# GpSimd computes the inverse square roots of the normalisations, in place of ScalarE's root and VectorE's reciprocal

## The reference

```
ln(x) = (x - mean) / sqrt(var + 1e-5)
x = x + tanh(g0) * cross_attention(ln(x), ctx)      # first attention, 16 heads
x = x + tanh(g1) * moe_64_experts(ln(x))            # top 8 of 64 experts, and a shared one
x = x + tanh(g2) * mlstm(ln(x), ctx)                # 16 heads; each head's output is normalised
                                                    #   h * rsqrt(var(h) + 1e-6) * scale
x = x + tanh(g3) * block(ln(x))                     # block: a = h + attention(ln(h)*w1+b1),
                                                    #   a + moe_4_experts(ln(a)*w2+b2)
```

## Time and profile before

| | |
|---|---|
| runs | 1759.97 us median of 3 |
| profiled execution, its own time | 1760.46 us |
| its span (first to last instruction) | 1759.2 us |
| TensorE busy | 1610.3 us, 92% |
| VectorE, ScalarE, GpSimd busy | 1101.2, 1007.2, 609.9 us |
| mean granted clock of TensorE | 0.946 of full |

### The profile page before, as it was taken

The page is one execution under the profiler, slowest core; times in us unless marked ns, Lnnn a source line. Parts: engine busy times, 40 slices in busy tenths (PEclk is TensorE's granted clock), DMA queues, the critical chain, the costliest instruction groups (busy, mean ns, idle before and its releaser), DMA issues.

```text
span 1759.2 us, 30253 instructions
## 1 busy us (share of the span) xinstructions
PE 1610.3 (92%) x10996; PEld 1269.9 (72%) x10996; DVE 1101.2 (63%) x2052; ACT 1007.2 (57%) x2050; POOL 609.9 (35%) x495
## 2 busy tenths in 40 slices
PE   4589999699999999999996984999999999999898
PEld 2245655388888888888872553788888888888687
DVE  6668886577544455444445566866876777666554
ACT  4368888444433344333335663877877876776543
POOL 5333333133435333333430002454454464443000
PEclk9589999899999999999995896999999999999899
DMA  5646665264433333334300003344344334332310
GB/s 157 194 143 200 205 203 161 88 148 111 108 105 105 107 113 107 105 105 115 112 9 8 4 2 128 104 149 162 114 139 122 123 121 134 121 115 67 72 49 25
DMA packets 111028, 196.16 MB, mean 112 GB/s; under 512 B 16712, under 2 KB 59532, under 8 KB 108064
## 3 DMA queue, kind: packets, MB, share of 16 engines
q1 hardware_dynamic: 110880, 194.21, 36.6%
HBM read 167.64 MB, written 25.73 MB: 110 GB/s over the span
## 4 chain that ended last, share of the span: by engine, by line
PE 78%; DVE 7%; ACT 5%; issue 4%; DMA 2%; POOL 2%; SPq 1%; ACTq 0%; POOLq 0%; DVEq 0%
PE bank L67 17%; PE bank L69 17%; PE bank L68 17%; PE bank L262 4%; PE bank L304 4%; PE bank L290 3%; PE bank L1790 3%; PE bank L1758 3%; PE bank L1780 1%; POOL e_hidden L1008 1%; PE bank L1290 1%; PE bank L1289 1%; PE bank L1300 1%; PE bank L1309 1%; PE bank L1754 1%
## 5 line engine op out<-in xcount | busy, mean ns | idle before, releaser
L1008 POOL TENSOR_TENSOR e_hidden<-e_gated,e_comb_wide 128x512 f32<-128x512 f32 x132 | 211.2, 1600 | 347.7 <-DVE e_gated L973 332.0
L848 ACT CAST e_hidden_hi<-e_hidden 128x512 fp32r<-128x512 f32 x132 | 82.0, 621 | 319.2 <-POOL e_hidden L1008 319.2
L966 DVE TENSOR_TENSOR e_hidden_lo<-e_hidden,e_hidden_hi 128x512 fp32r<-128x512 f32 x132 | 98.1, 743 | 212.1 <-ACT e_hidden_hi L848 212.1
L69 PE MATMUL bank<-e_x_hi,e_weights_lo 128*128 128x512 f32 (+1 forms) x528 | 209.8, 397 | 0.0
L67 PE MATMUL bank<-e_x_hi,e_weights_hi 128*128 128x512 f32 (+1 forms) x528 | 208.8, 395 | 0.7 <-ACT e_comb_rows L808 0.7
L68 PE MATMUL bank<-e_x_lo,e_weights_hi 128*128 128x512 f32 (+1 forms) x528 | 208.8, 395 | 0.0
L1869 ACT ACTIVATE b_turned<-bank,b_swap_bias 64x512 f32<-64x512 f32 x256 | 175.1, 684 | 44.0 <-PE bank L69 40.5
L481 DVE TENSOR_REDUCE a_negmax<-bank 128x2 f32<-128x512 f32 x256 | 164.5, 684 | 42.4 <-PE bank L262 41.2
L2018 POOL TENSOR_TENSOR b_turned<-b_turned,b_rope_q 128x512 f32<-128x512 f32 x64 | 82.7, 1292 | 255.8 <-ACT b_turned L1869 255.8
L398 ACT ACTIVATE a_exp<-bank 128x512 f32<-128x512 f32 x256 | 143.8, 596 | 30.1 <-PE bank L290 21.5
L69 PE MATMUL bank<-e_weights_hi,e_hidden_lo 128*128 128x256 f32 (+1 forms) x528 | 149.0, 282 | 0.0
(11 more groups left out here) (327 smaller groups left out, 4133.3 us busy)
## 6 DMA issues: line engine op xcount, KB each, us to landing
e_comb_wide<-e_combT SPq DMA_DIRECT2D x130, 256.0 KB, 4.0
e_raw<-in_e_weights SPq DMA_DIRECT2D x64, 384.0 KB, 4.5
b_qk_hi<-b_qk_parts SPq DMA_DIRECT2D x64, 256.0 KB, 2.7
b_qk_lo<-b_qk_parts SPq DMA_DIRECT2D x64, 256.0 KB, 3.0
a_qs<-a_q_parts SPq DMA_DIRECT2D x48, 192.0 KB
a_ks<-a_k_parts SPq DMA_DIRECT2D x48, 192.0 KB
b_qk_parts<-columns SPq DMA_DIRECT2D x32, 256.0 KB, 3.5
b_vw_hi<-b_v_parts SPq DMA_DIRECT2D x16, 512.0 KB, 4.1
```

Source lines behind the costliest of these rows:

```text
L69: return pe.matmul(out, w_lo, x_hi, start=False, stop=stop, skip_group_check=True)
L966: dve.tensor_tensor(lo[0:rows, :], m.hidden[at % 2][0:rows, :], hi[0:rows, :].bitcast(F32), ALU.subtract).then_inc(s.hidden_lo)
L1008: pool.tensor_tensor(m.hidden[i][0:rows, :], m.gated[i][0:rows, :], m.comb_wide[u % E_RING][0:rows, chunk * BANK:(chunk + 1) * BANK], ALU. ...
```

## The change

24 roots move: four of the router's norms, two column norms, two of the mLSTM's norms, four of the cells' factors (128x64), eight first and second norms of the block's attention and four of its gates. ScalarE's square root and VectorE's reciprocal go; GpSimd computes t to the power -0.5 in place, against a constant column of -0.5 that is spread over the free dimension. The semaphores keep their names: `root` now means that the inverse root is done, and is raised by GpSimd. The four norms ahead of the first attention stay as they are.

```
+def inverse_root(k, t):
+
+    return k.nc.gpsimd.tensor_tensor(t, t, k.minus_half[:, 0:1].to_broadcast([P, t.shape[1]]), ALU.pow)
 def layer0_pool(k, m, s, ring):
+    pool.memset(k.minus_half[:, :], -0.5).then_inc(own.tick())
 # experts_act, route and columns (the same in scan_act, cells_act, gate_act, attention_act)
-        if piece == 1:
-            act.wait_ge(s.var, chunk + 1)
-            act.activation(t.norm.rstd[:, :], t.norm.rstd[:, :], ACT.Sqrt).then_inc(s.root)
 # experts_dve, norm_end (the same in scan_dve, cells_dve, norm_end_dve)
-        dve.reciprocal(t.rstd[:, :], t.rstd[:, :]).then_inc(own.tick())
-        dve.wait_ge(own.sem, own.n)
 # experts_pool
+    def root(chunk):
+        pool.wait_ge(s.var, chunk + 1)
+        inverse_root(k, m.routers[chunk % HALF].norm.rstd[:, :]).then_inc(s.root)
     pool.wait_ge(before.added, NB)
+    for chunk in range(HALF):
+        root(chunk)
     for n in range(len(E_STEPS)):
         for chunk in range(HALF, NCHUNK):
+            if route_piece(chunk, n) == 1:
+                root(chunk)
+        for chunk in COLUMNS_AT:
+            if column_piece(chunk, n) == 1:
+                pool.wait_ge(s.column_var, chunk + 1)
+                inverse_root(k, m.columns_norm.rstd[:, :]).then_inc(s.column_root)
 # scan_pool
     pool.memset(first(w.drop), LOWEST).then_inc(s.resets)
+    for i, chunk in enumerate(LEFT):
+        pool.wait_ge(s.var, i + 1)
+        inverse_root(k, w.norms[chunk].rstd[:, :]).then_inc(s.root)
     pool.memset(m.log_gate[0:PARTS, :, :], 1.0).then_inc(s.log_ready)
 # cells_pool, for each group g, behind the weighing of its cells
+        pool.wait_ge(s.rooted, g + 1)
+        inverse_root(k, m.factor[g % 2][:, :, :].rearrange("p b h -> p (b h)")).then_inc(s.deviation)
 # gate_pool
+    if piece == 1:
+        pool.wait_ge(s.gate_var, chunk + 1)
+        inverse_root(k, m.norm.rstd[:, :]).then_inc(s.gate_root)
 # attention_pool
+        if piece in (1, 4):
+            pool.wait_ge(s.var, 2 * chunk + (piece == 4) + 1)
+            inverse_root(k, w.norm.rstd[:, :]).then_inc(s.root)
-    pool.wait_ge(s.small_in, 4 * DMA)
-    for piece in range(6, INPUT_PIECES):
+    for piece in range(INPUT_PIECES):
+        if piece == 9:
+            pool.wait_ge(s.small_in, 4 * DMA)
         input_chunk(0, piece)
```

More of the change, by code:

```diff
@@ L834, in experts_act @@
             piece = column_piece(chunk, n)
-            if piece == 1:
-                act.wait_ge(s.column_var, chunk + 1)
-                act.activation(m.columns_norm.rstd[:, :], m.columns_norm.rstd[:, :], ACT.Sqrt).then_inc(s.column_root)
             if piece in (3, 4):
@@ L1149, in scan_act @@
         keys_act(k, m, s, piece)
-    for i, chunk in enumerate(LEFT):
-        act.wait_ge(s.var, i + 1)
-        act.activation(w.norms[chunk].rstd[:, :], w.norms[chunk].rstd[:, :], ACT.Sqrt).then_inc(s.root)
     for half in range(2):
@@ L1351, in cells_act @@
         g, piece = divmod(n - M_LATER, CHUNK)
-        if g >= 0 and piece == 2:
-            act.wait_ge(s.rooted, g + 1)
-            act.activation(m.factor[g % 2][:, :, :], m.factor[g % 2][:, :, :], ACT.Sqrt).then_inc(s.deviation)
         if n < NB:
@@ L1420, in cells_dve @@
             dve.wait_ge(s.deviation, g + 1)
-            dve.reciprocal(factor[:, :, :], factor[:, :, :]).then_inc(own.tick())
-            dve.wait_ge(own.sem, own.n)
             dve.tensor_tensor(factor[:, :, :], factor[:, :, :], inv[:, :, :], ALU.mult).then_inc(own.tick())
@@ L1607, in gate_act @@
     act, cols = k.nc.scalar, slice(chunk * BANK, (chunk + 1) * BANK)
-    if piece == 1:
-        act.wait_ge(s.gate_var, chunk + 1)
-        act.activation(m.norm.rstd[:, :], m.norm.rstd[:, :], ACT.Sqrt).then_inc(s.gate_root)
     if piece in (3, 4):
@@ L1708, in norm_end_dve @@
 def norm_end_dve(k, t, src, dst):
-    dve, own = k.nc.vector, k.dve_steps
-    dve.reciprocal(t.rstd[:, :], t.rstd[:, :]).then_inc(own.tick())
-    dve.wait_ge(own.sem, own.n)
+    dve = k.nc.vector
     for b in range(CHUNK):
@@ L1833, in input_chunk @@
         cols = slice(chunk * BANK, (chunk + 1) * BANK)
-        if piece in (1, 4):
-            act.wait_ge(s.var, 2 * chunk + (piece == 4) + 1)
-            act.activation(w.norm.rstd[:, :], w.norm.rstd[:, :], ACT.Sqrt).then_inc(s.root)
         if piece in (6, 7):
@@ L2210, in program @@
         k.ident, k.gates = (stack.enter_context(nc.sbuf_tensor(n, s, F32)) for n, s in (("ident", [P, P]), ("gates", [P, 4])))
+        k.minus_half = stack.enter_context(nc.sbuf_tensor("minus_half", [P, 1], F32))
         k.columns_ready = [k.sem(f"columns_ready{chunk}") for chunk in range(NCHUNK)]
```

## The result

The changed kernel took 1776.49 us (median of 4 runs, 1768.84 to 1781.28) beside 1759.70 for the one before (4 runs, 1750.63 to 1762.73): ratio 1.0089, 95% interval 1.0052 to 1.0126. It is slower by 17 us. The forecast was 1734, and its range of 1726 to 1748 missed. The profiled execution took 1775.44 us for a span of 1774.1.

The account below looks back on a forecast made before the run. TensorE, busy 92% of the span, bounds the kernel; only its idle time or lowered clock counts. Terms -10.4, -12.5, +0.1, +0.2, -3.9, -0.7, +0.9 sum to -26.3 from 1760.5: forecast 1734 us, range 1726 to 1748.

Parts of the forecast that it names:

- its own price: Cost of a power on GpSimd, taken as ten multiplies per element: 1.5 us for 128x64, 0.5 for 128x4.
- slow rival: In the cells VectorE stands behind a slow 128x64 power; 1769 us at 10 us, decides from about 8 us; 7%.
- Inner groups: Cells: ScalarE goes straight to the exponentials, TensorE keeps 5.15 us steps and clock; -13.2, less 0.7 given back, -12.5 us.
- The lost clock: In the cells, with a 10 us power, each inner stall lowers the clock again, 2 us each.
- Last two groups: End of the cells, where nothing hides the power: +0.7 us each, less a load of 1.3 us; sum +0.1.
- First norms of the block: First two norms, TensorE idle: 0.5 us of power for a root and reciprocal of 0.2 each; +0.2 in all.
- Attention of the block: Roots and their table loads go, so TensorE's ten waits for the exponentials go; -10.4 us.
- what was to show it: Signs: 16 ScalarE loads, `b_probs` wait under 1 us, even cell steps at full clock, power near 1.5 us, others.
- The sign that was to warn: VectorE's L1423 waiting for GpSimd in the cells' inner groups would show the forecast wrong.
- Experts in the loop: Router norm's rows 1.5 us earlier: -2.2 us of TensorE waits, -1.7 of clock; sum -3.9.
- Ahead of the loop: First chunk's rows start earlier, without ScalarE in the chain, held by the first weights' split; -0.7 us.
- Start of the mLSTM: Powers push GpSimd's memset of `m_log_gate` among VectorE's rows, which end later; a loss of +0.9 us.

Follow-up runs that it names:

- experiments 2 and 4: 2: only the cells' four 128x64 powers, on the kernel before, 1791.84 us; 4: changed kernel plus spare operations ending GpSimd's stream, 1777.53 us in one run.
- experiment 1: Changed kernel with the cells' four 128x64 factors back on ScalarE's root and VectorE's reciprocal, the other 20 roots on GpSimd; 1742.84 us, ratio 0.989.
- experiment 3: Changed kernel with a GpSimd multiply in place of the cells' 128x64 power, leaving that root out; 1735.82 us, ratio 0.9857.
- experiment 6: Kernel before with only the roots of the block's attention and gates moved to GpSimd's power; 1749.86 us, ratio 0.9951.
- experiment 5: Changed kernel with the cells' power taken of half the tile, 128x32, leaving part of the root out; 1753.86 us, ratio 0.9965.

## Why the prediction was wrong

**The step that failed** is the first of "The change part by part", its own price: "I take ten multiplies per element, which is nearer the low rows: 1.5 us for 128x64". It is 96 multiplies and 10.52 us. No run shows how the power is computed inside. The range of the price did hold it (13 us for a hundred multiplies), and so did the slow rival, which puts its threshold at 8 us and got 7%. The estimate from the nearest rows was an estimate about another kind of operation: a multiply says nothing of what a power does per element, and "nearer the low rows" was no reason. With two bounds a factor of 40 apart and none of the middle shown, the case beyond 8 us deserved much more than 7%. That case was also said to want four times the multiplies taken; by its own figures, 60 against 10, it is six times.

The slow rival had the mechanism right: VectorE stands in order behind the power, most of it uncovered in the inner groups and all of it in the last. Its sum of 1769 us at 10 us becomes 1771 at 10.52 us; 1776.5 was measured.

The price goes into three terms. *Inner groups:* there are two of them and not the three of the prediction's heading (four in all, and the last two are counted apart); the sum went by the two long steps and isn't changed by it. The forecast hid 3.5 us of a power. Measured, 10.52 - 7.17 = 3.35, and with half the tile 5.41 - 2.06 = 3.35: that part was right. The lost clock, put at 2 us a stall, was 5.7 at the first and 1.6 at the second (13.89 us step, less 5.15 and 7.17), and 1.6 to 3.8 behind the same wait in experiments 2 and 4. The 13.2 us that were to be won here also came from one execution: its six steps took 44.1 us, those of experiment 1, with the same order, 40.7. *Last two groups:* 33.26 us against 12.78 with the multiply, a difference of 20.48, and 2 x (10.52 - 0.29) = 20.46 is the whole of it. *First norms of the block:* 1.01 us each in place of 0.5, so +1.2 and not +0.2.

**With the cells corrected the sum closes, in part by luck.** Cells and stretch behind them came to +27.9 for -12.4, 40.3 more; 1734.2 + 40.3 = 1774.5, and the profiled execution took 1775.4 (the median is 1776.5). But 4.4 us of the measured time are the first attention's, which the change doesn't touch, and they stand against the 3.3 us that the block's heads gave beyond their term. The better test is experiment 3: without the price it gives 1735.8, for a forecast of 1734.

**Attention of the block**, -10.4: right in the waits, and 0.9 to 3.3 too small in the whole, by busy time that goes with the waits (experiment 6). The measured waits were the better base: the estimate of some 20 us, from the drain that the Trainium skill (ScalarE: Activation LUTs, What ACT_TABLE_LOAD costs) adds to each load, doesn't agree with the 11.3 to 13.7 of the traces.

Of what was to show it, the 16 loads, the wait for `b_probs` (0.8 us in all) and the stretched rows came. The power near 1.5 us (10.52) and that of 128x4 near 0.5 (1.0 to 1.5), the even steps of the cells and the full clock there did not, nor did the wait of about 1 us for rows near 372, which went altogether. The sign that was to warn, VectorE's product behind the root (L1423, now L1426) waiting for GpSimd, came with 37.4 us in four waits, 16.1 of them in the inner groups.

**Experts in the loop**, -3.9: -3.9, but the tenth is luck. The waits for rows, 3.2 us, went altogether where 2.2 were booked, so 0.7 is left for the clock where 1.7 were booked. In experiment 6, with the experts' roots still on ScalarE, the first wait was 1.35 us and not 2.51, the clock stayed at 1.00, and the stretch took 120.4 us where the trace of before has 121.9. **Ahead of the loop**, -0.7: -0.7 here, but this stretch took 28.2 to 31.1 us in the traces with the powers there and 29.2 to 30.1 in those without, so it can't be told.

**Start of the mLSTM**, +0.9: the mechanism showed. VectorE's rows of both chunks and GpSimd's memset behind the second power:

```profile
924.95 4.23 DVE L1200 TENSOR_SCALAR m_norm_rows<-resid,m_norm_mean_var,m_norm_rstd 128x256 f32<-128x256 f32 x8
...
926.17 1.90 POOL L1251 MEMSET m_log_gate<- 3x2048 bf16 x1
```

Eight rows at 0.33 us apart would take 2.7 us and took 4.23; the last ends 8.1 us after the first statistics, where it was 6.95 before. The first chunk's rows escaped; the first row of the second chunk, at 926.40, took 1.82 us where the others took 0.41. All traces with these powers on GpSimd end the rows after 8.09 us, and all without them after 6.95. Its share in the time can't be told: the stage took 41.3 to 46.5 us in the profiled runs.

**What moved without the change.** The first attention, the same code in all, took 320.8 to 330.7 us in the profiled executions, and the wait in it that varied most is TensorE's for the transfer `a_qs<-a_mparts` (11.3 us before, 17.3 in two waits in experiment 5). The cells begin at the low clock in some executions, as in experiment 3. Runs of one kernel spread over 10 to 20 us, so 0.2% was too fine a bound for a comparison of a few runs: the intervals here are 0.2 to 0.5% to each side.

## What to carry to other kernels

The cost of an operation that no row shows can't be read off the rows of other operations on the same engine: where a sum rests on it, spread the chance over its whole range. A slow operation off the critical path is free only as long as nobody stands waiting for it. VectorE takes its instructions in order, so here the user of a 10 us power belongs two steps later, and where no later step exists, the root belongs on ScalarE, which takes 0.26 us for it. Taking ScalarE's table changes out of a loop in which TensorE waits for its exponentials was worth 11.3 to 13.7 us, 2 to 3 more than the waits themselves. A stage's time in one trace can be off by several us through the clock alone: the cells, with ScalarE's roots, took 83.9 to 88.3 us in four traces of three kernels, so a term should be read from more than one.

## What the runs showed of the hardware

- A power on GpSimd takes 160 ns per element of a partition (10.52 us for 128x64, 20.73 for 128x128), with exponents -0.5 and 2, values 1.7 and 1.0, and 32 and 128 partitions alike. From the rate that the Trainium skill (GPSIMD Engine Reference, Performance versus the Vector engine) gives for loops with data-dependent branches, the estimate was 0.6 us above the base for 128x64; the trace doesn't agree, with some 10.2.
- While the power runs, VectorE's products, which read one operand from a `bank` that TensorE wrote, are not slowed: four took 2.48 us beside the power, and 2.48 in experiment 3 without it. Other VectorE work beside it isn't shown. While GpSimd multiplies, VectorE can be slowed: L1426, 0.23 us alone, took 2.18 beside the weighing of 2.17 us that started at 1073.16.
- A wait of TensorE of 2.06 us in the cells was followed by the lower clock, while waits up to 2.3 us in the block's attention left the slices at 9 of 10 or more, and one of 1.00 us in the cells cost nothing more. A wait's length alone doesn't tell whether the clock falls, nor what it costs (1.5 to 6.0 us in the cells); what else decides isn't shown.
